# Routing a mixture of experts: logits taken from unscaled rows, beside their statistics

## The chip, the cores and the metric

One core of a Trainium2 chip runs the whole program in one launch. The metric is the device time in microseconds, the median of three runs. The engines are TensorE (PE), VectorE (DVE), ScalarE (ACT), GpSimd (POOL) and SyncE (SP, which issues DMAs). Each runs its own instruction stream in order, and they meet at semaphores.

## The reference

Four blocks act in turn on x, of 1024 tokens (4 batches of 256) with 256 features. The change is in the first two.

```python
x = x + tanh(g_xattn[0]) * L0_xattn(ctx, layernorm(x))   # top-76 mask of 256x256 similarities
x = x + tanh(g_ffn[0])   * L0_ffn(layernorm(x))          # 64 experts, top 8
x = x + tanh(g_xattn[1]) * L1_xattn(layernorm(x), ctx)
x = x + tanh(g_ffn[1])   * L1_ffn(layernorm(x))
# _L0_ffn:
logits = x @ gate_w.T                  # x is normalised here
probs = softmax(logits)
topk_w, topk_idx = top_k(probs, 8)     # combine weights are not renormalised
out = sum over experts e of combine[:, e] * (silu(x @ g_e.T) * (x @ u_e.T)) @ w2_e.T
```

## The kernel before

Routing works in steps b = 0 to 3, one per batch of 256 tokens (two tiles of 128). In a step, TensorE makes the similarities (`scores`), VectorE finds the 76th largest of each row by ten rounds of a maximum of eight and a replacement (`top_rounds`, L1110 and L1114) and writes the mask times the sigmoid (`mask`, L1142). TensorE adds the base, the mask and its transpose in PSUM (`mix`, L530 to L535), ScalarE copies the sum to X1 (L898). Then VectorE takes mean and variance (`mix_stats`, L1151), POOL takes the root of the variance (`norm_scale`, L434 and L436), VectorE scales the rows into XNA (`mix_norm`, L1163), TensorE flips XNA (L543), ScalarE copies it to XNT (L900), TensorE multiplies by the gate (L551), VectorE picks eight experts per token (`choose`, L1172 to L1178), TensorE counts how many earlier tokens took each expert (`ranks`, L560 and L561, one matmul per earlier tile of 128 tokens), and VectorE makes from this the slot of each token (`place`, L1185 to L1192: KEY, K8, IDX). ScalarE takes the exponentials of the logits (L906).

VectorE's order is written by hand in the main loop (L1199 to L1220): the rounds of step b + 1 fill the gaps between the parts of step b. POOL then issues 16 scatters per step (L447), one per tile and choice; each is an indirect DMA that writes 128 rows of XNA to 128 slots in `xs`. The root of step b + 1 stands behind ten scatters of step b (`POW_AT` = 2 in the second tile). Each expert has 192 slots, 64 experts 12,288 rows. SP fills them with zeros by twelve DMAs of 1 MB (L336) before the first scatter, and behind them loads the weights of the second layer (L340).

After step 3, TensorE counts the tokens of each expert (L576, L578), VectorE orders the experts by load (ORD), and SP loads the weights of the first eight experts (L348), waits for all scatters, and loads their slots (L352); every further expert is loaded when one of the eight buffers is free, slots ahead of weights. Meanwhile VectorE works out the combine weights (L1242 to L1286). The expert loop runs on TensorE (flip L593, gate and up L606, down L616). The second layer follows, with gathers by POOL.

These lines carry the order in SP's stream:

```python
first = [expert(e) for e in range(RING)]
for e in range(RING):
    load_weights(e, first[e])
sp.wait_ge(S["scattered"], 16 * TT * TOP0)
for e in range(RING):
    load_slots(e, first[e])
```

## Time and profile before

| | us |
|---|---|
| median of 3 runs | 563.95 (562.79 to 567.25) |
| profiled execution | 561.23 |
| its span, first to last instruction | 559.3 |
| TensorE busy | 412.9 (74%) |
| VectorE busy | 344.4 (62%) |
| ScalarE busy | 184.5 (33%) |
| POOL busy | 148.6 (27%) |
| POOL, 64 scatters (L447) | 64.9 busy, mean 1.014 |
| mean granted TensorE clock | 0.92 of full |

The busy shares are means over stages that have different limits. What an edit in routing is worth is read from the routing stage alone: which engine the last scatter waits for, and what that engine waits for. A row of a timeline gives the start, the duration, and in brackets how long the engine stood before it and what released it.

### The profile page before, as it was taken

The numbers are of one execution on the slowest core, as the hardware profiler recorded it, in microseconds if no ns is written. First come the engines' busy times: TensorE is split into PE (matmuls) and PEld (weight loads), VectorE is DVE, ScalarE is ACT, GpSimd is POOL, SyncE is SP. The second block draws the span as 40 slices with busy tenths as digits, with TensorE's granted clock in tenths as the row PEclk, the third lists the DMA queues.
The fourth block names the chain that finished last, engine by engine and source line by source line (L and its number), as shares of the span: only waits on it lengthen the run. The fifth ranks groups of instructions, "written<-read, shape, count | busy, mean of one in ns | idle before, by whom it ended". The sixth has DMA issues, their size and how long they took to land.

```text
span 559.3 us, 9235 instructions
## 1 busy us (share of the span) xinstructions
PE 412.9 (74%) x2738; PEld 347.8 (62%) x2738; DVE 344.4 (62%) x1053; ACT 184.5 (33%) x377; POOL 148.6 (27%) x156
## 2 busy tenths in 40 slices
PE   5345642500799999999823676799789988998796
PEld 3234441400798888988622554797678867996695
DVE  4988876279334444443346893488667885680664
ACT  3122220100233333343236143524453354427321
POOL 4017775757000000000477723330424000000000
PEclk9999999755699999999965879799999999999999
DMA  7999222237599999999832201110212000000000
GB/s 238 424 416 403 91 94 76 94 112 282 146 293 303 324 317 313 331 355 385 279 98 75 86 22 56 39 39 2 59 39 75 2 0 0 20 1 2 2 19 20
DMA packets 36789, 82.96 MB, mean 148 GB/s; under 512 B 6032, under 2 KB 16144, under 8 KB 34960
## 3 DMA queue, kind: packets, MB, share of 16 engines
q1 hardware_dynamic: 23616, 56.48, 29.2%
q0 software_dynamic: 6144, 16.79, 9.4%
q10 hardware_dynamic: 6992, 9.24, 4.6%
q8 instruction: 17, 0.28, 0.2%
q14 instruction: 20, 0.16, 0.1%
HBM read 50.44 MB, written 31.92 MB: 147 GB/s over the span
## 4 chain that ended last, share of the span: by engine, by line
PE 50%; DVE 13%; issue 12%; POOL 7%; ACT 7%; SPq 4%; DMA 3%; another core or an unknown queue 2%; ACTq 1%; DVEq 0%; POOLq 0%
PE PS L606 9%; POOL slots_in L447 7%; PE PS L616 6%; PE PS L695 5%; PE PS L772 3%; PE PS L708 3%; PE PS L709 3%; PE PS L710 3%; PE PS L593 2%; PE PS L669 2%; DMA XE<-slots_in 2%; PE PS L790 2%; PE PS L800 2%; PE PS L757 2%
## 5 line engine op out<-in xcount | busy, mean ns | idle before, releaser
L454 POOL DMA_INDIRECT GB<-slots_out,IDXG x64 | 70.2, 1096 | 221.1 <-DMA slots_out<-OE 133.3
L606 PE MATMUL PS<-XTE,WR 128*128 128x128 f32 (+2 forms) x512 | 80.5, 301 | 0.0
L447 POOL DMA_INDIRECT slots_in<-XNA,IDX x64 | 64.9, 1014 | 38.3 <-issue 30.8
L606 PEld LDWEIGHTS PS<-XTE,WR 128*128 128x128 f32 x512 | 71.2, 195 | 0.3
L1302 DVE TENSOR_TENSOR HE<-SGE,PS 128x128 f32<-128x128 f32 (+2 forms) x64 | 19.9, 312 | 71.7 <-ACT SGE L927 66.3
L616 PE MATMUL PS<-WR,HE 128*80 128x256 f32 (+2 forms) x198 | 53.3, 380 | 0.5 <-issue 0.5
L918 ACT COPY XTE<-PS 128x256 f32<-128x256 f32 (+2 forms) x64 | 26.3, 410 | 73.1 <-PE PS L593 72.0
L708 PE MATMUL PS<-XH,WGH 128*128 128x256 f32 x160 | 50.3, 314 | 0.0
L593 PE MATMUL PS<-CF,XE 80*128 80x80 f32 (+2 forms) x198 | 28.6, 258 | 26.2 <-DMA XE<-slots_in 26.0
L695 PE MATMUL PS<-WD,XW 128*128 128x256 f32 x160 | 42.6, 389 | 5.8 <-DVE TH L1391 5.8
L593 PEld LDWEIGHTS PS<-CF,XE 80*128 80x128 f32 (+2 forms) x198 | 22.9, 145 | 36.5 <-DMA XE<-slots_in 29.7
L709 PE MATMUL PS<-XL,WGH 128*128 128x256 f32 x160 | 45.5, 284 | 0.0
L710 PE MATMUL PS<-XH,WGL 128*128 128x256 f32 x160 | 45.4, 284 | 0.0
L1295 DVE COPY OE<-PS 128x256 f32<-128x256 f32 (+2 forms) x64 | 36.2, 566 | 8.2 <-PE PS L616 5.5
L979 ACT ACTIVATE AM<-PS 128x256 f32<-128x256 f32 x40 | 15.3, 383 | 68.9 <-PE PS L710 68.8
L1391 DVE SCALAR_TENSOR_TENSOR TH<-PS,CM,TH 128x256 f32<-128x256 f32 x72 | 31.5, 479 | 4.4 <-PE PS L695 3.9
L695 PEld LDWEIGHTS PS<-WD,XW 128*128 128x128 f32 x160 | 27.9, 193 | 9.2 <-DVE XW L1398 4.3
L927 ACT ACTIVATE SGE<-PS 128x128 f32<-128x128 f32 (+2 forms) x64 | 18.9, 296 | 43.9 <-PE PS L606 43.9
L616 PEld LDWEIGHTS PS<-WR,HE 128*80 128x80 f32 (+2 forms) x198 | 30.0, 165 | 5.2 <-issue 0.9
L1473 DVE TENSOR_REDUCE NM<-PS 128x2 f32<-128x256 f32 x64 | 31.6, 549 | 2.4 <-PE PS L775 2.2
L1347 DVE SCALAR_TENSOR_TENSOR BASE<-GB,W,BASE 128x256 f32<-128x256 f32 x56 | 26.7, 485 | 10.1 <-DMA GB<-slots_out,IDXG 5.5
L708 PEld LDWEIGHTS PS<-XH,WGH 128*128 128x128 f32 x160 | 30.9, 193 | 1.1 <-issue 0.6
(226 smaller groups left out, 814.9 us busy)
## 6 DMA issues: line engine op xcount, KB each, us to landing
WR<-in_wexp SPq DMA_DIRECT2D x64, 384.0 KB
slots_in<-GB SPq DMA_DIRECT2D x12, 1024.0 KB, 18.5
XE<-slots_in SPq DMA_DIRECT2D x24, 160.0 KB, 4.4
slots_out<-OE ACTq DMA_DIRECT2D x24, 160.0 KB
XE<-slots_in SPq DMA_DIRECT2D x29, 128.0 KB, 4.3
slots_out<-OE ACTq DMA_DIRECT2D x24, 128.0 KB
WGU<-in_wgu SPq DMA_DIRECT2D x1, 2560.0 KB
XE<-slots_in SPq DMA_DIRECT2D x11, 192.0 KB, 4.1
```

The costliest lines, as they stand in the source:

```text
L447: pool.indirect_dma_start(out=xs, out_offset=bass.IndirectOffsetOnAxis(ap=IDX[:, t, j:j + 1], axis=0), in_=XNA[:, t, :], in_offset=None, b ...
L454: pool.indirect_dma_start(out=GB[:, t % BT, j, :], out_offset=None, in_=ys[0:rows, :], in_offset=bass.IndirectOffsetOnAxis(ap=IDXG[:, t, j ...
L593: last = nc.tensor.transpose(psXE[place % 2][:, k, r * rows:(r + 1) * rows], XE[0:rows, place % RING, r, k * P:(k + 1) * P], ident[0:rows, ...
L606: last = mm(psGE[place % 2][:, a, 0:cap(place)], W13[:, k, a, :], XTE[:, place % 2, k, 0:cap(place)], start=(k == 0), stop=(k == KC - 1))
L616: last = mm(psOE[place % 2][0:rows, r, :], HE[:, place % 2, r * rows:(r + 1) * rows], WR[:, place % RING, 2 * D:3 * D], start=True, stop=True)
L695: last = mm(psW[:, t, :], H1[:, c % 2, t * P:(t + 1) * P], WD1[:, c, :], start=True, stop=True)
L708: mm(dst, WGH[:, c, k, a, :], XH[:, k, :], start=(k == 0), stop=False)
L709: mm(dst, WGH[:, c, k, a, :], XL[:, k, :], start=False, stop=False)
L710: last = mm(dst, WGL[:, c, k, a, :], XH[:, k, :], start=False, stop=(k == KC - 1))
L1295: V.tensor_copy(OE[0:rows, place % ORING, 0:parts, :], psOE[place % 2][0:rows, 0:parts, :]).then_inc(S["oe_copied"], 1)
L1391: last = V.scalar_tensor_tensor(FA[:, t, :], psW[:, t, :], w, so_far[:, t, :], ALU.mult, ALU.add)
L1473: last = V.tensor_reduce(NM[:, t, u * 2:(u + 1) * 2], ps1[:, u % 2, :, t * P:t * P + (t + 1) * P], AX.X, ALU.max, negate=True)
```

## The change

1. The flips take X1, not XNA, and wait for ScalarE's copy of X1. The gate is made to have mean zero over the features (`centre_gate`: TensorE sums it against a matrix of -1/256, VectorE adds the result to it), so the mean of a row drops out of the product. The scale of a row is positive and does not change which eight are the largest; the exponential takes it as its scale, and the bias is the largest logit times the scale, negated. The scales are kept per tile in RSN.
2. The root of the next step stands behind 12 scatters instead of 10. The rounds on VectorE are spread by `FIRST_ROUNDS` and `LATER_ROUNDS`.
3. The zeros are written in two parts: slots 0 to 127 of each expert by eight DMAs, slots 128 to 191 by four. The first tile's scatters wait for the first part only.
4. `ranks` uses a running sum of the masks of earlier steps (MSUM, made by VectorE behind `place`) in place of one matmul per earlier tile, and the two counts of step 3 stand ahead of its ranks.
5. `mix` adds both base products before it waits for the mask.
6. ScalarE makes the scores and the base of step b + 2 before the exponentials of step b.
7. SP loads the weights of three experts before it waits for the scatters; for experts 3 to 7 it reads the index, loads slots, then weights, after it.
8. The path that runs only when an expert has over 192 tokens flips XNA itself. It is not taken with these inputs.

```diff
@@ -57,9 +57,16 @@
...
-POW_AT = 2
+ROOT_BEHIND = 12
+LOW = 128
...
+AHEAD = 3
+FIRST_ROUNDS = (1, 2, 2, 3)
+LATER_ROUNDS = (3, 4, 4, 5)
 SIM_SCALE = 1.0 / 16.0
...
@@ -183,7 +190,10 @@
...
         LR = sb("LR", [P, BT, E0])
+        RSN = sb("RSN", [P, TT, 2])
+        MINUS_MEAN = sb("MINUS_MEAN", [P, P])
         MB = sb("MB", [P, TT, E0], BF16)
+        MSUM = sb("MSUM", [P, E0], BF16)
         FM = sb("FM", [P, 3])
...
@@ -332,9 +342,12 @@
...
             sp.wait_ge(S["zero_set"], 1)
-            for i in range(SLOTS // (8 * P)):
-                sp.dma_start(xs[i * 8 * P:(i + 1) * 8 * P, :].rearrange("(p r) d -> p (r d)", p=P), ZERO)\
-                  .then_inc(S["zeroed"], 16)
+            by_expert = xs.rearrange("(e c) d -> e c d", c=CAP)
+            for first, rows, signal in ((0, LOW, "zeroed_low"), (LOW, CAP - LOW, "zeroed")):
+                experts = P * 8 // rows
+                for e in range(0, E0, experts):
+                    sp.dma_start(by_expert[e:e + experts, first:first + rows, :].rearrange("e (q r) d -> e q (r d)", r=8),
+                                 ZERO).then_inc(S[signal], 16)
             for dst, src in ((WQ1[:, :, :, :], wq1), (WK1[:, :, :], wk1), (WV1[:, :], wv1), (WO1[:, :, :], wo1),
...
@@ -352,12 +365,17 @@
...
-            first = [expert(e) for e in range(RING)]
-            for e in range(RING):
+            first = []
+            for e in range(AHEAD):
+                first.append(expert(e))
                 load_weights(e, first[e])
             sp.wait_ge(S["scattered"], 16 * TT * TOP0)
-            for e in range(RING):
+            for e in range(AHEAD):
                 load_slots(e, first[e])
+            for e in range(AHEAD, RING):
+                n = expert(e)
+                load_slots(e, n)
+                load_weights(e, n)
             for e in range(RING, E0):
...
@@ -411,9 +429,10 @@
...
             nc.gpsimd.memset(MINUS_HALF[:, :], -0.5).then_inc(S["half_set"], 1)
+            nc.gpsimd.memset(MINUS_MEAN[:, :], -1.0 / D).then_inc(S["half_set"], 1)
             nc.gpsimd.memset(GB[:, 1, 6:, :], 0.0).then_inc(S["half_set"], 1)
-            pool.wait_ge(S["half_set"], 2)
+            pool.wait_ge(S["half_set"], 3)
...
@@ -431,19 +450,23 @@
...
                 pool.wait_ge(S["var_ready"], b + 1)
-                nc.gpsimd.tensor_scalar(RS[:, :, 3:4], MV[:, :, 1:2], EPS, None, ALU.add).then_inc(S["eps_added"], 1)
+                tiles = slice(b * BT, (b + 1) * BT)
+                nc.gpsimd.tensor_scalar(RSN[:, tiles, 1:2], MV[:, :, 1:2], EPS, None, ALU.add).then_inc(S["eps_added"], 1)
                 pool.wait_ge(S["eps_added"], b + 3)
-                nc.gpsimd.tensor_tensor(RS[:, :, 0:1], RS[:, :, 3:4], MINUS_HALF[:, 0:BT].unsqueeze(2), ALU.pow).then_inc(S["rs_ready"], 1)
+                nc.gpsimd.tensor_tensor(RSN[:, tiles, 0:1], RSN[:, tiles, 1:2], MINUS_HALF[:, 0:BT].unsqueeze(2), ALU.pow).then_inc(S["rs_ready"], 1)
...
             norm_scale(0)
-            pool.wait_ge(S["zeroed"], 16 * (SLOTS // (8 * P)))
+            pool.wait_ge(S["zeroed_low"], 16 * (E0 * LOW // (8 * P)))
             for t in range(TT):
+                if t == 1:
+                    pool.wait_ge(S["zeroed"], 16 * (E0 * (CAP - LOW) // (8 * P)))
                 pool.wait_ge(S["xn_ready"], t // BT + 1)
...
                 for j in range(TOP0):
-                    if t % BT == BT - 1 and j == POW_AT and t // BT + 1 < B:
-                        norm_scale(t // BT + 1)
+                    b = t // BT + 1
+                    if b < B and t % BT * TOP0 + j == ROOT_BEHIND:
+                        norm_scale(b)
                     pool.indirect_dma_start(out=xs, out_offset=bass.IndirectOffsetOnAxis(ap=IDX[:, t, j:j + 1], axis=0),
...
@@ -527,44 +550,63 @@
...
                 for t in range(BT):
-                    mm(psT[:, t, :], ident, BASES[b % 2][:, t, :], start=True, stop=False)
-                    if t == 0:
-                        pe.wait_ge(S["masked"], b + 1)
+                    mm(psT[:, t, :], ident, BASES[b % 2][:, t, :], start=(t == 0), stop=False)
+                pe.wait_ge(S["masked"], b + 1)
+                for t in range(BT):
                     mm(psT[:, t, :], ident, AM[:, t, :], start=False, stop=False)
                     for c in range(BT):
-                        last = mm(psT[:, t, c * P:(c + 1) * P], AM[:, c, t * P:(t + 1) * P], ident, start=False, stop=(c == BT - 1))
+                        last = mm(psT[:, t, c * P:(c + 1) * P], AM[:, c, t * P:(t + 1) * P], ident, start=False, stop=(t == BT - 1 and c == BT - 1))
                 last.then_inc(S["summed"], 1)
+            def centre_gate():
+                pe.wait_ge(S["half_set"], 3)
+                for k in range(KC):
+                    last = mm(psN, MINUS_MEAN[:, :], GATE0[:, k, :], start=(k == 0), stop=(k == KC - 1))
+                last.then_inc(S["gate_summed"], 1)
             def logits(b):
-                pe.wait_ge(S["xn_ready"], b + 1)
+                pe.wait_ge(S["x1_kept"], b + 1)
                 pe.wait_ge(S["xnt_copied"], b)
...
                     for t in range(BT):
-                        last = nc.tensor.transpose(psX[:, k, t * P:(t + 1) * P], XNA[:, b * BT + t, k * P:(k + 1) * P], ident)
+                        last = nc.tensor.transpose(psX[:, k, t * P:(t + 1) * P], X1[:, b * BT + t, k * P:(k + 1) * P], ident)
                 last.then_inc(S["xn_flipped"], 1)
...
                 pe.wait_ge(S["exp_done"], b)
+                if b == 0:
+                    pe.wait_ge(S["gate_centred"], 1)
                 for t in range(BT):
...
+                pe.wait_ge(S["idx_ready"], b)
+                if b:
+                    pe.wait_ge(S["masks_added"], b)
                 pe.wait_ge(S["mask_ready"], b + 1)
-                pe.wait_ge(S["idx_ready"], b)
-                for t in range(BT):
-                    n = b * BT + t
-                    for m in range(n):
-                        mm(psR[:, t, :], onesb, MB[:, m, :], start=(m == 0), stop=False)
-                    last = mm(psR[:, t, :], before, MB[:, n, :], start=(n == 0), stop=True)
+                own = [MB[:, b * BT + t, :] for t in range(BT)]
+                if b == B - 1:
+                    parts = [MSUM[:, :]] + own
+                    for i, part in enumerate(parts):
+                        mm(psN, onesb, part, start=(i == 0), stop=(i == BT))
+                    for i, part in enumerate(parts):
+                        mm(psC, part, onesb[:, 0:1], start=(i == 0), stop=(i == BT))
+                for t in range(BT):
+                    earlier = ([MSUM[:, :]] if b else []) + own[0:t]
+                    for i, part in enumerate(earlier):
+                        mm(psR[:, t, :], onesb, part, start=(i == 0), stop=False)
+                    last = mm(psR[:, t, :], before, own[t], start=(not earlier), stop=True)
                 last.then_inc(S["ranked"], 1)
...
             pe.wait_ge(S["loaded_gate0"], 48)
+            centre_gate()
             for b in range(B):
...
@@ -572,11 +614,6 @@
...
-            for n in range(TT):
-                last = mm(psN, onesb, MB[:, n, :], start=(n == 0), stop=(n == TT - 1))
-            for n in range(TT):
-                last = mm(psC, MB[:, n, :], onesb[:, 0:1], start=(n == 0), stop=(n == TT - 1))
-            last.then_inc(S["counted"], 1)
             pe.wait_ge(S["order_set"], 1)
...
@@ -900,14 +944,15 @@
...
                     base(1)
-                act.wait_ge(S["mask_ready"], b + 1)
-                for t in range(BT):
-                    n = b * BT + t
-                    last = A.activation(C0[:, n, :], psL[:, t, :], ACT.Exp, bias=SM[:, n, 0:1], accum_out=SM[:, n, 1:2])
-                last.then_inc(S["exp_done"], 1)
                 if b + 2 < B:
...
                     base(b + 2)
+                act.wait_ge(S["bias_ready"], b + 1)
+                act.wait_ge(S["rs_ready"], b + 1)
+                for t in range(BT):
+                    n = b * BT + t
+                    last = A.activation(C0[:, n, :], psL[:, t, :], ACT.Exp, scale=RSN[:, n, 0:1], bias=SM[:, n, 0:1], accum_out=SM[:, n, 1:2])
+                last.then_inc(S["exp_done"], 1)
             A.preload_act_table(ACT.Silu)
...
@@ -1160,7 +1208,7 @@
...
                 for t in range(BT):
-                    last = V.tensor_scalar(XNA[:, b * BT + t, :], X1[:, b * BT + t, :], MV[:, t, 0:1], RS[:, t, 0:1], ALU.subtract, ALU.mult)
+                    last = V.tensor_scalar(XNA[:, b * BT + t, :], X1[:, b * BT + t, :], MV[:, t, 0:1], RSN[:, b * BT + t, 0:1], ALU.subtract, ALU.mult)
                     if t < BT - 1:
...
@@ -1171,11 +1219,18 @@
...
                 st.wait()
-                st.done(V.tensor_scalar(SM[:, b * BT:(b + 1) * BT, 0:1], L8[:, :, 0:1], -1.0, None, ALU.mult))
                 for t in range(BT):
...
                 V.tensor_tensor(MB[:, b * BT:(b + 1) * BT, :], psL, LR[:, :, :], ALU.not_equal).then_inc(S["mask_ready"], 1)
+                V.scalar_tensor_tensor(SM[:, b * BT:(b + 1) * BT, 0:1], L8[:, :, 0:1], -1.0, RSN[:, b * BT:(b + 1) * BT, 0:1],
+                                       ALU.mult, ALU.mult).then_inc(S["bias_ready"], 1)
+            def centre_gate():
+                dve.wait_ge(S["gate_summed"], 1)
+                for k in range(KC):
+                    last = V.tensor_tensor(GATE0[:, k, :], GATE0[:, k, :], psN, ALU.add)
+                last.then_inc(S["gate_centred"], 1)
...
@@ -1190,38 +1245,48 @@
...
                 V.tensor_scalar(IDX[:, b * BT:(b + 1) * BT, :], K8[:, b * BT:(b + 1) * BT, :], -1.0, None, ALU.add).then_inc(S["idx_ready"], 1)
+                if b == 0:
+                    V.tensor_tensor(MSUM[:, :], MB[:, 0, :], MB[:, 1, :], ALU.add).then_inc(S["masks_added"], 1)
+                elif b < B - 1:
+                    dve.wait_ge(S["masks_added"], b)
+                    st.done(V.tensor_tensor(MSUM[:, :], MSUM[:, :], MB[:, b * BT, :], ALU.add))
+                    st.wait()
+                    V.tensor_tensor(MSUM[:, :], MSUM[:, :], MB[:, b * BT + 1, :], ALU.add).then_inc(S["masks_added"], 1)
...
             base_scale(0, slice(0, BT))
+            centre_gate()
             top_rounds(0, 6, ROUNDS)
...
                     coefficients(1, BT, TT)
+                to_stats, to_norm, to_choose, to_place = LATER_ROUNDS if b else FIRST_ROUNDS
                 if ahead:
                     dve.wait_ge(S["sim_copied"], b + 2)
-                    top_rounds(b + 1, 0, 2 if b else 1)
+                    top_rounds(b + 1, 0, to_stats)
                 mix_stats(b)
                 if ahead:
-                    top_rounds(b + 1, 2 if b else 1, 3)
+                    top_rounds(b + 1, to_stats, to_norm)
                 mix_norm(b)
...
                 if ahead:
-                    top_rounds(b + 1, 3, 5)
+                    top_rounds(b + 1, to_norm, to_choose)
                 choose(b)
                 if ahead:
-                    top_rounds(b + 1, 5, 6)
+                    top_rounds(b + 1, to_choose, to_place)
                 place(b)
                 if ahead:
-                    top_rounds(b + 1, 6, ROUNDS)
+                    top_rounds(b + 1, to_place, ROUNDS)
             st.end()
             st = Steps(dve, S["dve_w8"])
-            dve.wait_ge(S["counted"], 1)
+            dve.wait_ge(S["ranked"], B)
             experts = slice(0, E0)
```

## Rows read from the trace of the kernel before

**Rows 1.** The page: GB/s that all DMA engines moved, in 40 slices of 14 us.

```profile
GB/s 238 424 416 403 91 94 76 94 112 282 146 293 303 324 317 313 331 355 385 279 98 75 86 22 56 39 39 2 59 39 75 2 0 0 20 1 2 2 19 20
```

**Rows 2.** Stretches: us, each engine's busy us (instructions), granted clock, DMA share, GB/s.

```profile
104.00:148.00 44.00, 10.44 (x66) 9.18 (x67) 28.75 (x76) 3.93 (x10) 24.99 (x25) 0.51 0.52 176
...
136.00:140.00 4.00, 0.00 (x0) 0.00 (x0) 3.83 (x6) 0.00 (x0) 2.61 (x3) 0.50 0.27 98
...
148.00:152.00 4.00, 4.00 (x22) 3.77 (x22) 1.04 (x2) 1.21 (x3) 0.00 (x0) 0.82 0.00 0
...
160.00:260.00 100.00, 99.83 (x708) 88.52 (x707) 43.11 (x98) 34.46 (x98) 0.00 (x0) 1.00 0.99 327
```

**Rows 3.** The chain of waits in 60 to 145 us, shares by line.

```profile
by line: POOL slots_in L447 35.6%; issue 30.2%; another core or an unknown queue 5.9%; PE PS L551 4.7%; DMA XE<-slots_in 3.1%; DMA slots_in<-XNA,IDX 2.8%; PE PS L543 2.6%; PE PS L593 1.9%; DVE XNA L1163 1.8%; POOL RS L436 1.7%; DVE LR L1176
```

**Rows 4.** Timeline of POOL: start, us, line, operation, out<-in, idle before and its releaser.

```profile
43.22 1.25 POOL L447 DMA_INDIRECT slots_in<-XNA,IDX  x1 [11.14 <-issue]
...
66.47 0.97 POOL L447 DMA_INDIRECT slots_in<-XNA,IDX  x1 [1.75 <-issue]
...
91.44 0.97 POOL L447 DMA_INDIRECT slots_in<-XNA,IDX  x1 [3.77 <-DVE IDX L1192]
...
102.94 0.97 POOL L447 DMA_INDIRECT slots_in<-XNA,IDX  x1 [0.30 <-issue]
...
103.93 0.26 POOL L434 TENSOR_SCALAR RS<-MV 128x2 f32<-128x2 f32 x1
...
105.19 1.07 POOL L447 DMA_INDIRECT slots_in<-XNA,IDX  x1 [0.19 <-issue]
...
116.30 0.97 POOL L447 DMA_INDIRECT slots_in<-XNA,IDX  x1 [3.67 <-DVE IDX L1192]
...
136.12 1.14 POOL L447 DMA_INDIRECT slots_in<-XNA,IDX  x1 [0.30 <-issue]
...
137.56 0.97 POOL L447 DMA_INDIRECT slots_in<-XNA,IDX  x1 [0.30 <-issue]
```

**Rows 5.** Timeline of VectorE (DVE), steps 0 to 3 and after.

```profile
29.91 0.75 DVE L1151 BATCH_NORM_STATS2 ST<-X 128x6 f32<-128x256 f32 x2 [1.29 <-ACT X L898]
...
39.50 0.74 DVE L1110 MAX8 TOP<-WORK 128x8 f32<-128x256 f32 x2
...
40.95 0.28 DVE L1185 TENSOR_TENSOR KEY<-PS,CF 128x128 f32<-128x128 f32 x1
...
47.27 0.91 DVE L1142 SCALAR_TENSOR_TENSOR AM<-GB,TOP 128x256 f32<-128x256 f32 x2
...
64.41 0.28 DVE L1185 TENSOR_TENSOR KEY<-PS,CF 128x128 f32<-128x128 f32 x1
...
84.72 0.36 DVE L1172 MAX8 L<-PS 128x8 f32<-128x64 f32 x2 [0.97 <-PE PS L551]
...
85.72 0.29 DVE L1178 TENSOR_TENSOR MB<-PS,LR 128x128 bf16<-128x128 f32 x1
...
89.38 0.29 DVE L1185 TENSOR_TENSOR KEY<-PS,CF 128x128 f32<-128x128 f32 x1 [1.93 <-remote]
...
90.41 0.17 DVE L1192 TENSOR_SCALAR IDX<-K 128x16 int32<-128x16 f32 x1
...
105.10 0.74 DVE L1163 TENSOR_SCALAR XNA<-X,MV,RS 128x256 f32<-128x256 f32 x2 [2.08 <-POOL RS L436]
...
114.23 0.29 DVE L1185 TENSOR_TENSOR KEY<-PS,CF 128x128 f32<-128x128 f32 x1 [3.25 <-remote]
...
137.89 0.89 DVE L1281 TENSOR_TENSOR EQ<-KEY,K 128x512 f32<-128x512 f32 x1
```

**Rows 6.** Timeline of TensorE (PE), steps 0 and 2.

```profile
26.50 1.06 PE L530 MATMUL PS<-BASE,CF 128*128 128x256 f32 x2
...
27.35 1.06 PE L533 MATMUL PS<-AM,CF 128*128 128x256 f32 x2
...
80.92 1.11 PE L543 MATMUL PS<-CF,XNA 128*128 128x128 f32 x4 [4.63 <-DVE XNA L1163]
```

More of the change, by code:

```diff
@@ L631, in all_tokens @@
             def all_tokens():
+                for b in range(B):
+                    pe.wait_ge(S["xnt_copied"], B + b)
+                    for k in range(KC):
+                        for t in range(BT):
+                            last = nc.tensor.transpose(psX[:, k, t * P:(t + 1) * P], XNA[:, b * BT + t, k * P:(k + 1) * P], ident)
+                    last.then_inc(S["xn_flipped"], 1)
+                pe.wait_ge(S["xnt_copied"], 2 * B)
                 with pe.Fori(0, E0 // 2) as i:
@@ L945, in all_tokens @@
                         act.wait_ge(gathered[t][j], 16)
+                for b in range(B):
+                    act.wait_ge(S["xn_flipped"], B + b + 1)
+                    A.copy(XNT[:, :, b * N:(b + 1) * N], psX).then_inc(S["xnt_copied"], 1)
                 with act.Fori(0, E0) as e:
@@ L1178, in choose @@
                 V.tensor_tensor(MB[:, b * BT:(b + 1) * BT, :], psL, LR[:, :, :], ALU.not_equal).then_inc(S["mask_ready"], 1)
+                V.scalar_tensor_tensor(SM[:, b * BT:(b + 1) * BT, 0:1], L8[:, :, 0:1], -1.0, RSN[:, b * BT:(b + 1) * BT, 0:1],
+                                       ALU.mult, ALU.mult).then_inc(S["bias_ready"], 1)
+            def centre_gate():
+                dve.wait_ge(S["gate_summed"], 1)
+                for k in range(KC):
+                    last = V.tensor_tensor(GATE0[:, k, :], GATE0[:, k, :], psN, ALU.add)
+                last.then_inc(S["gate_centred"], 1)
             def place(b):
```

4 lines of the change are left out of this document (2 added, 2 removed).

## The prediction

> **What bounds the kernel now.** I read the page first: its GB/s line shows the DMA engines near 420 GB/s in three slices (14 to 56 us) and near 90 for five more [rows 1]. The table of stretches then separates three stages [rows 2]: routing, until GpSimd (POOL) has issued the last scatter; the experts, where TensorE is busy 99.83 us of 100; and the second layer, which the change does not touch. In the chain of waits from 60 to 145 us POOL's scatter line has 35.6% and "issue" 30.2% [rows 3], so the timeline of POOL was read next [rows 4]. It issues 64 scatters in four batches of 16, one batch per step b. One scatter takes 0.97 us and the next begins 1.278 us after it (from 91.44 to 102.94 are nine such pitches). The batches begin at 43.22, 66.47, 91.44 and 116.30, so the periods are 23.25, 24.97 and 24.86 where 16 pitches and one root need 16 x 1.278 + 1.0 = 21.45. The 1.0 is what the root (two small POOL operations, starting at 103.93) puts between two scatters: 105.19 - 102.94 = 2.25 against 1.278. The rest of a period is POOL standing, 3.77 and 3.67 us with VectorE's IDX (L1192) named as the releaser [rows 4].
>
> The timelines of VectorE and TensorE say why IDX is late. After the root comes the scaling XNA, then flips, copy, logits, choice, ranks, IDX, all in series: root at 103.93, XNA at 105.10, KEY at 114.23 [rows 4, 5]. And KEY of batches 2 and 3 waited for something the profile cannot name ("remote", 1.93 and 3.25 us) [rows 5].
>
> **The change, part by part.**
>
> *Logits beside the root.* Flips now wait for ScalarE's copy of X1, not for XNA. From X1's end to logits' end is what the flips, the copy and the logits took: L543 at 80.92 to the first MAX8 of the choice at 84.72, 3.80, and 0.05 for the start: 3.85 [rows 5, 6]. The root's result is only needed by XNA and Exp, but VectorE runs in order: XNA(b) stands before choose(b) and place(b), and waits for a root that now lies behind 12 scatters of the batch before instead of 10. So the loop is: root start, +1.17 XNA, +0.65 choice starts (if the logits are there), +1.21 mask (84.72 to 86.01, less the 0.08 of the operation that moved), +0.10 for the bias operation, +1.45 one round (39.50 to 40.95), +1.20 KEY to IDX's end (89.38 to 90.58), +0.86 to the scatter (90.58 to 91.44): 6.64 us [rows 4, 5]. POOL meanwhile has four scatters: the first 1.26 after the root's start, 1.37 for it (1.07 long), then 3 x 1.278: 6.46 until it could issue the next batch. It stands 0.18 us, not 3.7. A period is 21.45 + 0.18, 21.65 us.
>
> *First batch.* Centring the gate costs two VectorE operations on 128x64 with a PSUM input. KEY's addition, 128x128, took 0.28; I take 0.18 each, 0.35 in all, on VectorE's path to the first mask (bounds 0.2 and 0.6, all of KEY's time for each). Its TensorE half, two matmuls of the logits' kind, comes while VectorE is still in the rounds of batch 0. Moving the second base product ahead of the mask's wait takes one L530 pair off the path: 0.85 [rows 6]. X1(0) reached VectorE's statistics at 29.91 [rows 5]; now its copy ends at 29.4. Logits end at 33.25. VectorE fits in statistics, one round, XNA and the second part of base_scale by then; choice 1.3, a round 1.45 and 1.2 give IDX at 37.4, against 42.14 (first scatter 43.22 less 1.08). First scatter: 38.4. *Zeroing* covers this: inputs 1.87 MB (the shapes of the nine loads ahead) plus the low 8.39 MB make 10.26 MB; the GB/s line has moved 9.27 MB by 28 us and the rest takes 2.4 us, so the low part is there at about 30.4 and the whole at 40.5 [rows 1]. The second token tile is scattered from 48.6. Cost nothing; without the cover (low part at the old end) the first scatter would be at 41.5. The eight plus four issues are as many as the twelve before.
>
> *Second batch.* Here VectorE is the limit: from IDX(0) the mask sum 0.2, six rounds 8.65, the last MAX8 0.72, mask 0.15 + 0.90 [rows 5] give 48.0; mixing 3.8 (4.65 less 0.85), X1 copy 0.63, statistics 1.0 (0.75 and 0.25) reach 53.4. The root's slot behind 12 scatters is 53.7. XNA 54.9, logits 56.2, then 1.21 + 0.10 + 1.45 + 1.20 + 0.86: scatter at 61.0 (POOL free at 60.1). Third batch 61.0 + 21.65 = 82.65. The mask sums (0.2 to 0.45 us per batch, bounded by two KEY additions, 0.58) lie behind IDX; VectorE has statistics ready at 73.7 where the root's slot is 76, so 2.3 us of cover; if it goes they add themselves.
>
> *Ranks.* Before, steps 0 to 3 had 3, 7, 11 and 15 matmuls; now 3, 5, 5 and, with both counts moved ahead, 11. The unnamed wait: with 3 and 7 matmuls KEY (40.95, 64.41) has no idle before it, so they were done behind the one round (1.45); with 11 it came 3.37 behind the mask (86.01 to 89.38), and with 15 it stood 3.25 [rows 5]. Step 2 falls to a count that showed none; step 3 keeps 11. So I charge it in full at step 3: bounds 0 and 3.3 there, 0 and 1.9 at step 2. Root at 97.7, XNA 98.9, mask 100.75, KEY 104.0, IDX 105.2, fourth batch at 106.0 (104.2 without the wait). Before it was 116.30: **10.3 us earlier**.
>
> *Last batch and SP's order.* The last 16 scatters took 116.30 to 138.53, 22.2 us, where 16 pitches are 20.4. In 136:140 the DMA engines were busy only 0.27, and still the scatter at 136.12 took 1.14, and VectorE's two-input EQ at 137.89 took 0.89 [rows 2, 4, 5]. So it is not the weight traffic that stretches them but VectorE's work, which moves along: I keep 22.2, and give five fewer weight loads nothing (bounds 0 and 1.8 gained). The Trainium skill, page "SBUF — State Buffer", section on the two separate sides, says that a VectorE instruction with two SBUF inputs and a GpSimd instruction that reads SBUF lock each other out. By that the 1.8 us stay, as I took them; by a contention of DMAs they would go. By that rule each of the five mask additions can hold one scatter too, for as long as it runs.
> The five weights (1.97 MB) now come after the scatters, each behind its slots. The DMA engines moved nothing in 148:152 while TensorE worked [rows 2], so most of it (1.3 of 1.97 MB at 327 GB/s in 4 us) fits in a hole, and the fourth expert comes third in TensorE's queue after the start. Taken: 0. Bounds 0 and 6.0 (1.97 MB at 327 GB/s).
> TensorE's granted clock is 0.51 over 104:148 and 0.82 in 148:152, after a long idle [rows 2]; the idle is as long afterwards, so its cost stays.
>
> **Sum.** First batch 4.8 earlier, second 5.5, third 8.8, fourth 10.3; nothing given back: -10.3 us. The profiled execution took 561.23 (span 559.3), 2.7 under the median of 563.95. It would be 550.9, the median **553.6**. With the small terms' bounds 551.8 (no unnamed wait) to 556.1 (step 2's 1.9 in full, and 0.55 of VectorE's).
>
> **Rivals.**
> *A, the experts give it back.* DMA share is 0.99 in 160:260 [rows 2]: a backlog entered there never goes. For it: that share. Against: TensorE's 99.83 of 100 with eight experts' buffers ahead. Price 6.0: 559.6.
> *B, a further wait takes the place.* Unnamed waits at steps 2 and 3 in full (1.9 more), the first scatter at 41.5 for the zeros (POOL's second batch then at 41.5 + 20.7 + 1.0 = 63.2, 2.2 more), the VectorE terms at their ends (0.55): 5.65 us left, 558.3. For it: the cause of "remote" is unknown. Against: steps 0 and 1.
> *C, slower: the root is too deep.* Place: XNA(b), which stops VectorE's queue until the root behind 12. If the logits still end only after XNA and its followers, as now, POOL stands 3.7 + 2 x 1.278 = 6.3 us a period, 2.55 more than now in three periods, 7.65, with nothing won in the first: 571.6. It decides when the logits (X1 plus 3.85) end over 3.3 us after XNA's 0.65: then a period is as long as now. I have them 0.65 us after it in the second batch (56.2 against 55.55) and 1.2 before it in the third. This is also the case in which the overlap does not come about.
> *D, more:* no unnamed wait, scatters of the last batch at 1.278: 1.8 + 1.8 more, 550.0.
>
> **Numbers.** Forecast 0.58, A 0.16 and B 0.09 (each half under 1%), C 0.06, D 0.11. A measurement of this kernel tells about 1% (5.6 us) from no change. Faster: 0.58 + 0.11 + half of A and B, 0.81; same 0.13; slower 0.06. Range 549.5 to 559.5: C, A's end and D's, under 0.2, are left out.
>
> **What would show it.** POOL's timeline: batches at 38.4, 61.0, 82.7, 106.0, and gaps between them under 1 us except the last; XNA starting right behind the root while L543 already ran; KEY(2) within 1.6 us of its mask, KEY(3) 3.3 behind; low zeros no releaser; the last 16 scatters 22 us; TensorE's first expert 10 us earlier and its expert stage as long as before. I am wrong if a period exceeds 23 us, if TensorE waits for WR of experts 3 to 7, or if the first scatter waits for the zeros.

## The result and the profile after

| | before | after |
|---|---|---|
| median, us (4 runs each) | 564.32 (562.79 to 567.25) | 579.82 (579.65 to 580.41) |
| profiled execution, span | 561.23, 559.3 | 579.66, 577.8 |
| mean granted TensorE clock | 0.92 | 0.841 |
| first scatter | 43.22 | 57.49 |
| end of the last scatter | 138.53 | 155.26 |
| first flip of an expert | 142.85 | 159.47 |
| first gather after the experts | 272.07 | 288.26 |

The change makes the kernel slower, by a ratio of 1.0285 (95% interval 1.0251 to 1.032). The forecast was 553.6. The shift is 16.7 us at the end of the scatters and 16.2 at the first gather, so nearly all of it arises in routing, and nothing is given back or lost among the experts (129.2 us from the first flip to the first gather before, 128.8 after). The lower granted clock does not make this difference: another execution of before, profiled later, has 0.857 and takes 563.21 us.

The page's GB/s line (40 slices of 14.4 us), against [rows 1], shows it first:

```profile
GB/s 199 210 286 272 373 194 78 85 98 147 99 271 335 327 319 320 306 355 374 379 131 89 75 38 38 36 56 20 40 37 73 19 2 0 18 2 3 2 19 18
```

Where the old kernel moves near 420 GB/s in slices two to four, this one moves 210 to 286. The stretch 14 to 26 us, when only the zeros run, is the cleanest reading (us, each engine's busy us and instructions, clock, DMA share, GB/s); before had 1.01 and 425 there:

```profile
14.00:26.00 12.00, 3.32 (x9) 2.23 (x8) 11.75 (x48) 2.46 (x4) 0.00 (x0) 1.00 0.51 209
```

The 16 DMA engines together are busy half the time, with work queued: SyncE spends 32.53 us on the issue of the twelve. The timelines of POOL and VectorE (start, us, line, out<-in, idle before and its releaser) say who pays:

```profile
57.49 1.25 POOL L470 DMA_INDIRECT slots_in<-XNA,IDX  x1 [26.13 <-DMA slots_in<-GB]
69.82 0.97 POOL L470 DMA_INDIRECT slots_in<-XNA,IDX  x1 [2.12 <-DMA slots_in<-GB]
81.17 0.97 POOL L470 DMA_INDIRECT slots_in<-XNA,IDX  x1 [0.35 <-issue]
107.56 0.97 POOL L470 DMA_INDIRECT slots_in<-XNA,IDX  x1 [0.46 <-issue]
133.04 0.97 POOL L470 DMA_INDIRECT slots_in<-XNA,IDX  x1 [4.27 <-DVE IDX L1247]
154.29 0.97 POOL L470 DMA_INDIRECT slots_in<-XNA,IDX  x1 [0.30 <-issue]
```

```profile
36.42 0.17 DVE L1247 TENSOR_SCALAR IDX<-K 128x16 int32<-128x16 f32 x1
75.83 0.73 DVE L1211 TENSOR_SCALAR XNA<-X,MV,RSN 128x256 f32<-128x256 f32 x2 [21.86 <-POOL RSN L456]
97.30 0.43 DVE L1158 MAX8 TOP<-WORK 128x8 f32<-128x256 f32 x1 [1.62 <-remote]
128.56 0.36 DVE L1220 MAX8 L<-PS 128x8 f32<-128x64 f32 x2 [4.05 <-remote]
```

IDX of step 0 is ready at 36.6, but POOL waits for the low zeros until 57.5. The root of step 1 lies behind twelve scatters, so VectorE stands 21.86 us at XNA: in-order queues pass the lateness on in full. The first batch is 14.3 us later than before and the last one 16.7 later ([rows 4] against these). The rest is of another kind. A handoff is the moment at which an operation starts because another, on another engine or on its own, has finished. Here some start long after that, and the profile names no releaser for the wait ("remote"); below, such a wait is called unnamed. ScalarE's copy of X1 in step 2 is one: TensorE's last product before it is modelled to end at 93.3, so 4.0 of the 10.42 us are lateness and the rest is ordinary waiting.

```profile
97.32 0.59 ACT L942 COPY X<-PS 128x512 f32<-128x512 f32 x1 [10.42 <-remote]
```

### The profile page after: what moved, and what is told of

The parts are those of the page before. It is cut to its first block, busy times and chain, and to the rows that moved or that the text cites. A ratio compares the mean times of both kernels' runs of the same rounds, so it can differ in the third digit from the quotient of the medians.

```text
span 577.8 us, 9201 instructions
## 1 busy us (share of the span) xinstructions
PE 411.7 (71%) x2714; PEld 347.7 (60%) x2714; DVE 344.8 (60%) x1060; ACT 185.1 (32%) x377; POOL 147.9 (26%) x157
## 4 chain that ended last, share of the span: by engine, by line
PE 52%; DVE 13%; issue 8%; DMA 7%; ACT 6%; SPq 6%; POOL 3%; another core or an unknown queue 2%; ACTq 1%; DVEq 0%; POOLq 0%
PE PS L643 12%; PE PS L653 7%; DMA slots_in<-GB 6%; SPq L349 5%; PE PS L739 5%; PE PS L630 3%; PE PS L713 3%; POOL slots_in L470 3%; PE PS L816 2%; PE PS L752 2%; PE PS L754 2%; PE PS L753 2%; DVE TOP L1158 2%; DVE WORK L1162 2%
## 5 line engine op out<-in xcount | busy, mean ns | idle before, releaser
L1063 ACT ACTIVATE PP<-PS 128x384 f32<-128x384 f32 x64 | 27.1, 491 | 14.1 <-PE PS L846 13.4
```

## The experiments

**1. One cause: the shape of the zero DMAs.** The low part's target is `e q (r d)` with 8 experts slowest, the high part's has 16. Experiment one turns the low part's order round; the bytes, the sizes and the number of DMAs stay.

```diff
-  ...rearrange("e (q r) d -> e q (r d)", r=8)
+  ...rearrange("e (q r) d -> q e (r d)" if first == 0 else "e (q r) d -> e q (r d)", r=8)
```

> The changed kernel with one edit: the eight DMAs of the low zeros give the 16 groups of 8 rows as their slowest dimension and the 8 experts as the next, instead of the other way round; same bytes, same 8 KB pieces, same gaps. Theory T (the slowest dimension of 8 spreads such a DMA over 8 of 16 engines, so it moves at half rate): the low part is there at about 31 us, the first scatter begins at IDX plus 0.9, 37.5 us, and the kernel takes 551 to 557 us. Rival R (the destination with a gap after every 128 KB is slow to write by itself): the low part comes at 57 us as before, 580 us. Rival S (issuing twelve such DMAs costs SP 32.5 us): issue stays 32 us, 580 us.

Two others share its chip. One gives before only the split zeroing of after:

```diff
-  for i in range(SLOTS // (8 * P)): ...      # 12 contiguous DMAs
+  for first, rows, signal in ((0, LOW, "zeroed_low"), (LOW, CAP - LOW, "zeroed")): ...
```

> The kernel before with only the zeroing of the changed kernel (eight DMAs of 8 experts x 16 groups for the low part, four of 16 x 8 for the rest, the first tile waiting for the low part only). If the zeroing alone is the cause of the loss (T, R and S all say so): first scatter at 57 us instead of 43.2, total 574 to 580 us. If another part of the change makes the loss (the root behind 12, the granted clock that fell at 28 us): 564 to 568 us.

The other gives after the twelve contiguous DMAs and the one wait of before:

> The changed kernel with the zeroing of the kernel before (twelve DMAs of one contiguous MB, one wait for all). T and R: zeros complete at 40.5 to 42 us, first scatter at 41.5 to 43, 552 to 558 us. If the loss lies elsewhere: 575 us or more.

And a dose: the low part in 16 DMAs of half a MB, four experts slowest (one execution):

```diff
-  experts = P * 8 // rows
+  experts = 4 if first == 0 else P * 8 // rows
```

> The changed kernel with the low part in sixteen DMAs of half a MB, each with 4 experts as the slowest dimension; same bytes and pieces. T: 4 engines each, a quarter of the rate, the low part at about 85 us or later, total about 605 us or more. R: as in the changed kernel, 57 us and 580. S: a third more issues, some 75 us.

| kernel | us | ratio to before | first scatter | DMA share, GB/s in 14 to 26 us |
|---|---|---|---|---|
| before | 564.26 | | 43.22 | 1.01, 425 |
| order turned round | 563.7 | 1.0003 [0.996, 1.0046] | 37.74 | 1.01, 425 |
| before with the split | 579.61 | 1.0262 [1.0219, 1.0305] | 58.58 | 0.50, 212 |
| after, contiguous zeros | 568.71 | 1.0071 [1.0008, 1.0133] | 42.90 | 1.01, 425 |
| four experts slowest | 614.66 | | 93.78 | 0.25, 106 |

The same stretch of the turned order and of the fours:

```profile
14.00:26.00 12.00, 3.32 (x8) 2.16 (x8) 11.75 (x48) 2.53 (x4) 0.00 (x0) 1.00 1.01 425
```

```profile
14.00:26.00 12.00, 3.31 (x8) 2.18 (x8) 11.75 (x48) 2.50 (x4) 0.00 (x0) 1.00 0.25 106
```

Shares of 1.01, 0.51 and 0.25 for 16, 8 and 4 in the slowest dimension are what 16, 8 and 4 of 16 DMA engines at full work would give. The change's own high part, with 16 slowest, is at full work as soon as the low part is out of the way, in 58 to 68 us of after:

```profile
58.00:68.00 10.00, 0.00 (x0) 0.00 (x0) 0.00 (x0) 0.00 (x0) 7.57 (x8) 0.50 1.00 367
```

The gaps in the target stay when the order is turned round, so they are not the cause; nor is SyncE's time for the issue by itself, which is still 17.58 us then, against 8.92 in before, with the low part there in time. The split alone costs before nearly as much as the whole change cost (1.0262 against 1.0285). This cause is shown. The Trainium skill, page "DMA: Bandwidth & Descriptors", section "Why a DMA increments its semaphore by 16 and not by 1", has the rule: the number of engines is the largest up to 16 that divides the slowest dimension (of more than 1) of both access patterns. The three shares agree with it.

But with the zeros mended the kernel takes as long as before: the forecast 10 us do not come, neither with the order turned round (551 to 557 expected, 563.7 measured) nor with contiguous zeros (552 to 558 expected, 568.71 measured). TensorE's logits of step 1 and VectorE's choices of steps 1 and 2 in the first experiment:

```profile
54.17 1.97 PE L582 MATMUL PS<-GATE,XNT 128*128 128x64 f32 x8 [1.44 <-issue]
```

```profile
60.67 0.36 DVE L1220 MAX8 L<-PS 128x8 f32<-128x64 f32 x2 [5.65 <-remote]
...
85.37 0.36 DVE L1220 MAX8 L<-PS 128x8 f32<-128x64 f32 x2 [3.02 <-remote]
```

The logits of step 1 end at 56.14 as modelled; the choice could start at 56.2 and starts at 60.67, 4.5 us late. In step 2 it is 3.8 late (logits' end 81.53, choice 85.37). POOL then stands 6.09, 3.81 and 3.72 us for IDX before batches 2 to 4 (65.37, 90.42, 115.38).

**2. What the late handoffs come with.** Four kernels keep the steps and change what POOL or SyncE does beside them. First, only the roots during the steps, all 64 scatters after step 3:

```diff
-  norm_scale(0)
+  for b in range(B): norm_scale(b)
   ...
+  pool.wait_ge(S["idx_ready"], B)
   for t in range(TT):                        # 64 scatters
```

> The first experiment's kernel (expert dimension not the slowest), but POOL does only the four roots during the steps and all 64 scatters come after step 3. Its total is longer and says nothing. Theory (unnamed waits come with POOL's indirect DMAs): TensorE's, VectorE's and ScalarE's handoffs in steps 1 to 3 show no wait for a remote releaser (at most 1 us in all, against 13 to 18 us), no root is late (each begins within 1 us of its statistics), and IDX(3) is there at 95 to 100 us, with steps of 19 to 21 us set by VectorE. Rival (the waits belong to the place in the instruction streams, such as late instructions): they stay at the same choices and keys, in multiples of about 1.65 us, over 6 us in all, and IDX(3) comes after 105.

Then with other work in their place: fills of a spare tile by POOL, plain DMAs by SyncE, plain DMAs by POOL.

```diff
+  nc.gpsimd.memset(FILL[:, :], 0.0)          # fills, 16 per step
+  sp.dma_start(ys[256 rows], XNA[two tiles]) # SyncE, 8 per step
+  pool.dma_start(ys[128 rows], XNA[a tile])  # POOL, 16 per step
```

> As the kernel with late scatters, but in steps 0 to 2 POOL fills a spare SBUF tile 16 times per step where the scatters stood. If POOL's being busy (its SBUF port, its place in the order) makes the unnamed waits, they return: over 5 us. If it takes its DMAs, there are none, and IDX(3) comes when the roots let it, some 4 to 8 us after the kernel with late scatters or less.

> As the kernel with late scatters, but in steps 0 to 2 SyncE issues, one after the other, 8 plain DMAs per step of 256 KB from XNA to the DRAM tensor of expert rows (unused at that time): the same bytes as the scatters, from a hardware queue and in long descriptors. If any DMA traffic makes the unnamed waits, they return: over 5 us. If it takes POOL's indirect DMAs, none over 1 us in all, and IDX(3) comes at the same time as in the kernel with late scatters.

> As the late scatters, but in steps 0 to 2 POOL issues 16 plain DMAs per step of 128 KB (a tile of XNA to the unused DRAM tensor of expert rows) where the scatters stood. If the unnamed waits belong to POOL's own queue they return, over 5 us; if to the indirect form (a row address for each of 128 descriptors), there are none over 1 us in all and IDX(3) comes by 100 us.

And half the dose, only the first tile's 8 scatters in each step:

> A dose between the first experiment and the late scatters: 8 indirect DMAs (the first tile's) instead of 16 in each step, the other 32 after step 3; total longer and of no meaning. If each indirect DMA under way gives a handoff a chance to be late, the unnamed waits are fewer, some 3 to 8 us in all against about 13 to 20, and fall only while scatters are being issued. If it takes a queue of them that never empties, there are none (under 1 us).

| kernel (one profile each) | unnamed waits, us | third IDX, end | fourth scatter batch can start |
|---|---|---|---|
| 16 scatters per step (experiment one) | 13.2 in VectorE, 2.8 in ScalarE | 89.4 | 115.38 |
| none | 0 | 78.5 | 99.24 |
| fills | 0 | 81.8 | 104.67 |
| SyncE's DMAs | 0 | 78.6 | 99.37 |
| POOL's plain DMAs | 0 | 79.1 | 98.58 |
| 8 scatters per step | 0 | 78.3 | 98.85 |

Choice, KEY and IDX of step 3 in the kernel without scatters beside them:

```profile
94.54 0.36 DVE L1217 MAX8 L<-PS 128x8 f32<-128x64 f32 x2 [0.76 <-PE PS L579]
...
96.96 0.29 DVE L1237 TENSOR_TENSOR KEY<-PS,CF 128x128 f32<-128x128 f32 x1 [1.13 <-PE PS L599]
...
98.00 0.17 DVE L1244 TENSOR_SCALAR IDX<-K 128x16 int32<-128x16 f32 x1
```

Both waits have TensorE as the releaser and are short; the forecast charged this KEY with 3.25. The label alone could mislead, so I also compare starts with modelled ends: in the five kernels below the first row of the table, every choice for which VectorE stood starts 0.03 to 0.04 us after its logits. So the late handoffs come neither from POOL being busy nor from DMA traffic (SyncE's moved as many bytes), and they were there with 16 indirect DMAs in a step and not with 8. POOL's plain DMAs leave a question open: one took 0.53 us, so the 12 in a row lasted under 7 us, less than the 10 of eight scatters. Whether it takes the indirect form, or any long run of POOL's DMAs, is not shown. The fills' last start comes later because each step's root waits for them, as expected.

**3. Run length or number.** Each run of 8 waits until the scatters ahead of it have landed, and the root stands behind 8 (`ROOT_BEHIND = 8`):

```diff
+  if j == 0 and t:
+      pool.wait_ge(S["scattered"], 16 * t * TOP0)
```

> The kernel with the root behind 10, with two edits on POOL: before each run of 8 scatters (one tile's) it waits until all earlier ones have landed, and the root of the next step stands behind 8. All 64 stay in the steps. If the unnamed waits need a long run of indirect DMAs without a pause (they were absent with runs of 8 and 9 us of pause, and none began less than 6 us into a run, most 12 or more), they are gone or under 3 us in all, VectorE's steps fall to 19 to 22 us, and POOL sets the period: 16 pitches, a root and two landings of about 2 us, some 24: the total stays at 558 to 564. If they follow the number of scatters per step whatever the pauses, they stay at 8 to 13 us beside the landings, and the total is 566 to 572.

No unnamed wait is left, and no choice is late, with all 64 scatters in the steps. That speaks for the length of the run and against the number per step. It does not settle it: the run was made on a chip (number 3) on which before takes 556.2 us, not 562 to 564, and no late handoff was seen in either kernel profiled there. The time, 570.3 us, lies in the range written down for the other outcome, and that for the one the trace shows (558 to 564) was too low. A boundary between two runs costs POOL 2.3 us, with the root in it or without:

```profile
71.61 0.97 POOL L472 DMA_INDIRECT slots_in<-XNA,IDX  x1 [2.32 <-DMA slots_in<-XNA,IDX]
...
81.53 0.26 POOL L454 TENSOR_SCALAR RSN<-MV 128x2 f32<-128x2 f32 x1
...
83.77 1.07 POOL L472 DMA_INDIRECT slots_in<-XNA,IDX  x1 [1.17 <-DMA slots_in<-XNA,IDX]
```

The ratio is 1.0215 [1.0119, 1.031], and the last scatter ends at 147.3, 9 us behind before's: the pauses cost more than the late handoffs did. VectorE now waits for POOL, 8.75 us at XNA of step 2.

**4. What the loop is worth with them.** The root behind 10, and on top of it three edits: VectorE makes the root itself by Newton steps; SyncE's order of before; the overlap alone undone.

```diff
-ROOT_BEHIND = 12
+ROOT_BEHIND = 10
```

> The first experiment's kernel with the root behind 10 scatters, as before, not 12. If the deeper root costs (rival C), each step's chain from the root starts 2 x 1.28 us sooner and POOL stands 2.5 us less per period in steps 2 and 3: 563.7 falls by 5 to 7 us, to 557 to 559, the periods to about 22.5. If the unnamed waits set the period whatever the root does, they take the place and the total stays within 2 us of 563.7.

It came out between the two, at 561.19: 2.5 us less, not 5 to 7.

> The kernel with the root behind 10, but the root is made by VectorE itself, by a guess and three Newton steps (11 small operations, about 2 us per step), so that POOL issues scatters alone and VectorE never stands for POOL. If the in-order chain POOL root to IDX to POOL was what gave the unnamed waits their price, steps then take VectorE's own 20 to 22 us plus the unnamed waits of 2 to 5, they hide behind 20.4 us of scatters, and the last scatter ends at 124 to 131 us against 136 in the kernel with the root behind 10: the total is 549 to 556, faster than both kernels. If VectorE with unnamed waits stays the limit whatever POOL does, periods stay at 24 to 25 and the total within 3 us of 561.

> The kernel with the root behind 10 and SyncE's order of before (all eight experts' weights ahead of the wait for the scatters). The prediction gave the order nothing (bounds 0 and 6.0 lost by the new order, 0 and 1.8 gained in the last batch). By it the total is within 2 us of 561.2 and the last 16 scatters take 22 us with eight weight loads as with three. If five fewer weight loads shorten the scatters, this kernel's last batch is 1 to 2 us longer; if the new order costs the experts, this kernel's expert stage is shorter by up to 6.

```diff
-  transpose(psX..., X1[...])   # behind x1_kept
+  transpose(psX..., XNA[...])  # behind xn_ready; Exp without scale, bias without scale
```

> The kernel with the root behind 10, with the overlap alone undone: TensorE flips XNA (after its scaling) as before, the exponential has no scale and the bias none. The forecast's loop gives a step's chain from the root 2.9 us more (3.85 of flips, copy and logits behind XNA in place of about 0.65 to the choice), in steps 1 to 3 and about 1.2 in the first: the overlap alone is worth about 1 us in batch one and up to 2.5 a period, 6 to 9 us in all, so this kernel takes 567 to 570. If the unnamed waits swallow the overlap (a handoff that starts earlier is late by as much), the total is within 3 us of 561.

The last one ran on chip 3, whose before took 556.2 us. So it ran again beside three others on chip 0, before's median 563.98 there:

> The kernel before, profiled once more beside the next two on one chip. In the run of the kernel with the overlap undone no handoff was late, and that chip ran before in 556.2 us, not 562 to 564. If the late handoffs belong to the execution or the chip and not to the program, this profile shows them in the next two kernels as well or in none of the three; before's batches then begin near 43, 66, 91, 116 with 5 us of unnamed waits, or up to 5 us earlier without them.

> The kernel with the root behind 10, again, on the chip of its two neighbours. If no handoff is late there, batches begin at 38, 60.5, 82.5, 105 (period 22, POOL-bound) and the last scatter ends at 127: 8 to 10 us faster than the kernel with the overlap undone and than before. If handoffs are late as in its first run (three, 8 to 12 us in all), it ends the last scatter at 133 to 137 and takes 0.996 to 0.998 of before.

> The kernel with the overlap undone, again. If it is free of late handoffs by its order (its flips and choices follow VectorE's scaling, at other moments of a run of scatters), it ends the last scatter at 134 to 135 again and takes 0.998 to 1.002 of before. If it was the chip, it shows late handoffs of 3 us and more now wherever the others do, and takes up to 1.01 of before.

> The first experiment's kernel (root behind 12) beside the one with the root behind 10. By rival C it is slower by 2 x 1.28 us in each of three periods less what POOL stands anyway, up to 7 us; by the forecast's loop the two differ by under 1 us without late handoffs; the ratios to before so far, 1.0003 and 0.9967 on two chips, lie 2 us apart.

| kernel | us, first time (chip) | ratio | us, side by side (chip 0) | ratio |
|---|---|---|---|---|
| root behind 12 (experiment one) | 563.7 (8) | 1.0003 [0.996, 1.0046] | 564.15 | 1.0028 [0.9987, 1.007] |
| root behind 10 | 561.19 (0) | 0.9967 [0.9941, 0.9994] | 561.12 | 0.9947 [0.991, 0.9985] |
| and overlap undone | 555.84 (3) | 0.9999 [0.9952, 1.0045] | 562.0 | 0.9967 [0.9931, 1.0002] |
| and VectorE's own root | 563.09 (12) | 1.003 [1.0003, 1.0056] | | |
| and SyncE's old order | 559.79 (12) | 0.9956 [0.9917, 0.9995] | | |

Three things follow. First, the late handoffs come back when the program runs again, and their largest sites with them. The choice of step 1 with the root behind 12, on its second chip, stands where it stood on the first (60.67, 5.65):

```profile
61.08 0.36 DVE L1220 MAX8 L<-PS 128x8 f32<-128x64 f32 x2 [5.74 <-remote]
```

So does KEY of step 3 (3.84 us, 4.55 the first time). Others move: ScalarE's copy of XNT is late in step 1 here and in step 2 there. And a label can hide one. The choice of step 2 starts 3.9 us after its logits' end here too, but the profile puts the wait down to "issue":

```profile
85.75 0.36 DVE L1220 MAX8 L<-PS 128x8 f32<-128x64 f32 x2 [3.04 <-issue]
```

ScalarE's copy of X1 in step 2 with the root behind 10, in its first profile and in its second, both on chip 0, starts 4.7 and 2.6 us after the mix's end, less than the bracket, which holds the ordinary waiting too:

```profile
76.33 0.59 ACT L942 COPY X<-PS 128x512 f32<-128x512 f32 x1 [11.06 <-remote]
```

```profile
75.40 0.59 ACT L942 COPY X<-PS 128x512 f32<-128x512 f32 x1 [10.29 <-remote]
```

The kernel before, profiled again, has them at KEY once more, as in [rows 5], and at step 1 too. Its batches begin at 43.07, 68.23, 93.35 and 118.32, the last 2.0 us later than in the profile that the prediction read:

```profile
66.16 0.29 DVE L1185 TENSOR_TENSOR KEY<-PS,CF 128x128 f32<-128x128 f32 x1 [1.82 <-remote]
...
91.27 0.29 DVE L1185 TENSOR_TENSOR KEY<-PS,CF 128x128 f32<-128x128 f32 x1 [1.04 <-remote]
...
116.25 0.29 DVE L1185 TENSOR_TENSOR KEY<-PS,CF 128x128 f32<-128x128 f32 x1 [3.37 <-remote]
```

Second, with the overlap undone no wait is unnamed, in either profile. But in the second one (chip 0) the choice of step 2 stands 5.61 us where in the first (chip 3) it stands 3.85, with TensorE named in both; 1.3 us of that lie between the logits' end and the choice. KEY of step 3 stands 1.82 where it stood 1.13.

```profile
84.98 0.36 DVE L1220 MAX8 L<-PS 128x8 f32<-128x64 f32 x2 [3.85 <-PE PS L582]
```

```profile
86.69 0.36 DVE L1220 MAX8 L<-PS 128x8 f32<-128x64 f32 x2 [5.61 <-PE PS L582]
```

So this kernel is not free of late handoffs by its order, and it ends its last scatter at 134.7 on chip 3 and at 137.45 on chip 0, where 134 to 135 were expected again. One program without late handoffs on one chip and with a few on another: the chip may have a part in them, and no kernel that shows them elsewhere was profiled on chip 3.

On chip 0 the kernel with the overlap undone loses 3.1 us in the first batch (IDX at 40.0 against 36.9), yet its 137.45 stands against 136.37 for the kernel with the overlap. There the overlap is worth 0.9 us of median, and the intervals overlap, where 6 to 9 were expected. By the profiles, what the overlap wins is lost again in handoffs that are late with it and less so without; that these follow from the overlap's earlier start is not shown. (On chip 3 the kernel without the overlap was level with its before.)

Third, taking POOL out of the root's chain gains nothing. The total is that of the second of the two outcomes written down for it; the periods are longer than either had them. Its batches begin at 39.97, 67.43, 94.75 and 119.54, and POOL stands for IDX:

```profile
94.75 0.97 POOL L459 DMA_INDIRECT slots_in<-XNA,IDX  x1 [7.16 <-DVE IDX L1251]
```

Even two operations of VectorE that follow each other were apart there:

```profile
57.76 0.16 DVE L1207 SCALAR_TENSOR_TENSOR RSN<-RS,RSN 128x2 f32<-128x2 f32 x1 [0.89 <-DVE RS L1205]
```

The kernel with the root behind 10 and the zeros' order turned round is some 3% under the change as it was made, and 0.5% and 0.3% under before in two sets of runs. Both intervals end under 1, but so small a gain is less than the 1% that the prediction calls a difference. With SyncE's old order it is as good.

## Why the prediction was wrong, step by step

**Zeroing: the step that failed.** "Zeroing covers this ... cost nothing" rested on a sum of bytes at 424 GB/s: low part there at 30.4. The bytes were right and the rate was not. I counted the DMAs (eight plus four, as many as twelve) and their sizes, and never asked over how many DMA engines one of them spreads. The low part landed at 57.5, 27 us later. The listed sign ("if the first scatter waits for the zeros") came true; rival B priced it at 3.1 us in the first scatter, since its bound was the old end of all zeros. With the order turned round the first scatter is at 37.74, 0.7 ahead of the forecast.

**First batch: right.** IDX was forecast for 37.4, and is there at 36.6.

**The period: failed too, by itself enough to lose the gain.** 21.65 was forecast; with the zeros mended the periods are 27.6, 25.05 and 24.96. The chain's own terms were about right: without scatters beside it step 3 takes 6.25 us from its root at 91.92 to IDX's end at 98.17, where my terms give 5.8 without the unnamed wait and 7.5 with it (97.7 to 105.2), and the fourth batch could start at 99.24 against 106.0. What failed is "I charge it in full at step 3". The unnamed wait is not tied to the ranks or to a count of matmuls. It can sit in any handoff, TensorE's to VectorE and ScalarE and VectorE's to itself, beside a long run of scatters. Most handoffs there are on time all the same: VectorE's combine work beside before's last 16 scatters shows no gap. In the first experiment the choices of steps 1 and 2 stand 5.65 and 3.02 for theirs and KEY of step 3 4.55.

**Rival C.** Its condition was that the logits end over 3.3 us after XNA's 0.65. In step 1 of the first experiment the choice starts 5.65 us after XNA's followers, and POOL stands 6.09, where C had 6.3. In steps 2 and 3 it stands 3.8 and 3.7. So what C describes is there, though by a late handoff and not by late logits, and at its full price in one period of three. Behind 10 scatters instead of 12 the kernel takes 0.9947 of before and not 1.0028, on one chip: 3 us, where the forecast's loop gave under one.

**Right:** the last 16 scatters take 22.2 us, also with three weight loads instead of eight beside them. With eight put back (SyncE's old order) they take from 113.71 to 135.93, 22.2 again:

```profile
113.71 0.97 POOL L470 DMA_INDIRECT slots_in<-XNA,IDX  x1 [4.15 <-DVE IDX L1247]
...
134.96 0.97 POOL L470 DMA_INDIRECT slots_in<-XNA,IDX  x1 [0.30 <-issue]
```

By the two-input rule of the Trainium skill, page "SBUF — State Buffer", section on the two separate sides, the stretching should stay and by a contention of DMAs it should go; it stayed. The kernel with all 64 scatters after step 3 shows the same more sharply. While VectorE's combine work lasts, to 124.90, ten of the 17 scatters behind the first take 1.12 to 1.46 us; all 46 after it take 0.97:

```profile
123.70 1.32 POOL L467 DMA_INDIRECT slots_in<-XNA,IDX  x1 [0.30 <-issue]
125.33 0.97 POOL L467 DMA_INDIRECT slots_in<-XNA,IDX  x1 [0.30 <-issue]
```

SyncE's order is worth nothing that shows, 0.9956 against 0.9967 of before, and the experts give nothing back (rival A). KEY of step 2 has no idle before it, as the fewer rank matmuls should have it; step 3's waits 1.14 in after.

**Open.** What makes a handoff late. Instruction fetches are rare in the traces (four packets in 50 to 96 us of the first experiment, as many in the kernel without scatters in its steps) and none lies at its late sites, so they are an unlikely cause. TensorE's granted clock does not part the kernels: over 40 to 100 us it is 0.53 in the first experiment and 0.53 in the kernel with the overlap undone on chip 3, which has no late handoff, and 1.00 in before, which has one in that stretch. The kernel with the overlap undone has runs as long as the others, so a long run is not enough. Whether it is needed, against a number of scatters per step, rests on the kernel with pauses alone, and so on chip 3. I did not try a change of the semaphores themselves.

## What to carry to other kernels

Before splitting or reshaping a DMA, read the slowest dimension of each side: keep it at 16 or, by the rule cited, a multiple of it, and check the DMA share of a stretch in which that DMA runs alone, since a share of 0.5 with work queued was half the rate here. A wait that the profile cannot name need not belong to the instruction that shows it. So a plan that moves handoffs beside the same neighbour should carry it into every one of them, as a case with a chance and a price. Such waits are better counted from the releaser's modelled end than by the label: two here were put down to "issue" and to TensorE. And where three queues hand over in a ring, a forecast needs one run with the neighbour taken away: it says at once whether the chain or its company is slow.

## What the runs showed of the hardware

- Plain DMAs whose target has 8, or 4, as its slowest dimension kept the 16 DMA engines at a share of 0.51, or 0.25, against 1.01: 209 and 106 GB/s against 425, with the same 1 MB (or half) each and the same element runs of 8 KB.
- Some handoffs between engines (TensorE to VectorE and ScalarE, VectorE to itself) were late by 0.9 to 5 us in long runs of indirect DMAs from POOL, a new one every 1.28 us. There were none in runs of eight, beside plain DMAs of POOL (48 of 128 KB, landing 2.3 us after issue, in runs of under 7 us), beside plain DMAs of SyncE, or beside fills; and none in one profile, on another chip, of a kernel with long runs.
- Scatters took 0.97 us each, and 1.12 to 1.46 in many cases beside VectorE's combine work, with three and with eight weight loads beside them.
- A scatter of 128 rows lands so that POOL, waiting for it, stands 2.3 us after the last issue.
